# A graph-message kernel on one core: a third of the node normalization goes to GpSimd, and its source gathers get another gate

## The chip, the core and the metric

The kernel runs on one core of a Trainium2 chip. The metric is device time in microseconds, the median of several executions. Engines: TensorE (PE), VectorE (DVE), ScalarE (ACT), GpSimd (POOL), and SyncE (SP), which here only issues DMAs.

## What is computed

25,000 edges send messages between 100,000 nodes of 128 features, all float32. `dst` is sorted.

```python
src, tgt = (x[row], x[col])
msg_input = jnp.concatenate([src, tgt, edge_attr], axis=-1)
h = jax.nn.relu(msg_input @ W1 + b1)
msg = h @ W2 + b2
attn_weight = jax.nn.sigmoid(jnp.concatenate([msg, conf], axis=-1) @ Wa + ba)
out = jax.ops.segment_sum(msg * attn_weight, col, num_segments=x.shape[0])
x = _layernorm(x + out, axis=-1)   # over the 128 features, eps 1e-5
```

Every node is normalized, the many without a message too.

## The kernel before, in words

**Edges.** 49 steps (`STEPS`, index k) of 512 edges (four groups of 128) each. 16 are *near* steps, for edges with low target numbers: their target rows come by plain DMA and a one-hot matmul ("pick"), and their sums go into a block `near` in SBUF ("place"). 33 are *list* steps: GpSimd gathers source rows (L658) and target rows (L669) by indirect DMAs, four of each in a step; sums run along each partition and land in `stash`, from where GpSimd scatters finished rows to `out` (L679, four DMAs for a list step, from step 15 on; the last eleven list steps' scatters come behind step 48's gather). `RING` = 4 buffers hold the gathered rows.

In step k TensorE turns (transposes) source rows, target rows and edge attributes into PSUM (L878, L883 or L892, L897); each of the three raises `turned_ps_ready` by one. ScalarE copies them to SBUF (L758), TensorE does the hidden layer (L904), ScalarE relu (L763), TensorE the messages (L914). VectorE adds biases (L1383, L1386), ScalarE does the sigmoid and gates (L767, L773), and VectorE (list) or TensorE and VectorE (near) sum. TensorE's order is written out: hidden(k), sums of k-1, turn(k+1), messages(k). ScalarE's: relu(k), turn(k+1), norms, gates(k), norms.

**Nodes.** All nodes beyond the near block pass through SBUF in 63 chunks of 128 partitions x 11 rows, three chunks to a batch b, one batch in two steps, 21 batches. Six slots (`SLOTS`) hold them, so a batch reuses the slots of the one two back. SP loads a chunk (L485), VectorE takes statistics (L1187), `batch_scales(b)` on VectorE works out two scalars a row in step 2b (L1168 to L1179; `sc` has two halves, used in turn), and the rows are normalized in place. `ACT_ROWS = (7, 7, 8)` says how many of each chunk's 11 rows ScalarE does (L777, `norm_chunk`); VectorE does the rest (L1229, `norm_rows`). `normed` counts 2 for a chunk when both are done. SP then stores it (L543) and, once that has landed, reloads the slot.

**SP** goes through one list in order. In iteration k, once turn(k) has ended: attributes of k+4, near loads for k+3 and k+2; in an even k reloads of chunks 0 and 1 of batch k/2+1, near blocks, then the store of chunk 2 of batch k/2-1; in an odd k the reload of chunk 2 of batch (k+1)/2, then the stores of chunks 0 and 1 of batch (k-1)/2.

**GpSimd** also has one list: 115 groups of four indirect DMAs: gathers of steps 0 and 1, then for each k from 2 the source gather, the target gather if k is a list step, and the scatters that `SCATTERS` puts there. `gather_src(k)` waits until the first part of turn k-4 is done (the buffer is free). In every second group, ahead of its third DMA (its second in a group behind a scatter), `pause` waits until the group before has landed.

Of the kernel before, what the change touches and what calls it, by code (L numbers as in the profile page):

```python
# [15 lines left out]
RING = 4  # L16
SLOTS = 6
# [53 lines left out]
HEAD_STEP = {l: STEP_OF[(S_, LG * (l + 1) - 1)] + 1 for l in range(LISTS)}  # L71
TAIL_STEP = {l: STEP_OF[(S_, LG * l)] + 1 for l in range(1, LISTS)}
V_STEP = 7
ACT_ROWS = (7, 7, 8)
NEAR_ACT = 6
BESIDE = 8
SSTEPS = 9
# [12 lines left out]
def is_list(k):  # L90
    return 0 <= k < K and STEPS[k][0] == S_
# [35 lines left out]
EXTRAS = [u for u in USES if u[0] != D_]  # L127


def list_groups_of(b):  # L130

    return [STEPS[k - 1][1] for k in (2 * b - 1, 2 * b) if is_list(k - 1)]
# [16 lines left out]
def columns(b):  # L149

    at, n = {}, 0
    if 3 * b < 63:
        at["nodes"] = n
        n += even(ROWS) + (2 * ROWS if crosses(b) else 2 * even(ROWS))
    for i in list_groups_of(b):
        at[i] = n
        n += G
    if b in NEAR_OUT:
        at["near"] = n
        n += even(NEAR_OUT[b][1] - NEAR_OUT[b][0])  # L160
    return at, n


COLS = [columns(b)[0] for b in range(BATCHES)]
WIDTH = [columns(b)[1] for b in range(BATCHES)]
WIDEST = max(WIDTH)
# [15 lines left out]
def build(nc, x, src, dstw, attr, conf, W1, b1, W2, b2, Wa, ba, out):  # L182
# [9 lines left out]
    with ExitStack() as ctx:  # L192
# [234 lines left out]
        def wait(eng, semaphore, value):  # L427
            if value > 0:
                eng.wait_ge(semaphore, value)
# [188 lines left out]
        def _(pool):  # L618
# [21 lines left out]

            def pause(j):
                landed, value, behind = latest
                if j == behind and groups[0] % PAUSE == PAUSE - 1:
                    pool.wait_ge(landed, value)

            def group_begun(landed, value, behind):
                groups[0] += 1
                latest[:] = landed, value, behind

            def gather_src(k):  # L650
                kind, i = STEPS[k]
                if k >= RING:

                    pool.wait_ge(turned_ps_ready, 3 * (k - RING) + 1)
                idx = table(src_list, i) if kind == S_ else src_near[:, i * G:(i + 1) * G]
                for j in range(G):
                    pause(j)
                    pool.indirect_dma_start(  # L658
                        out=rows_src[:, k % RING, j, :], out_offset=None, in_=x[:, :],
                        in_offset=bass.IndirectOffsetOnAxis(ap=idx[:, j:j + 1], axis=0),  # L660
                    ).then_inc(src_got[k % RING], 16)
                group_begun(src_got[k % RING], 16 * G * (k // RING + 1), 2)
# [89 lines left out]
        @block.scalar  # L752
        def _(act):
            def turn(k):
                for c in range(3):

                    act.wait_ge(turned_ps_ready, 3 * k + c + 1)
                    act.activation(turned[:, k % 2, c], turn_ps[:, c], ACT.Copy).then_inc(turned_ready, 1)  # L758

            def relu(k):  # L760

                act.wait_ge(hid_ps_ready, k + 1)
                act.activation(hid[:, k % 2], hid_ps[:], ACT.Relu, bias=b1_col[:, 0:1]).then_inc(hid_ready, 1)  # L763

            def gates(k):
                act.wait_ge(logit_ready, k + 1)
                act.activation(weight[:, k % 2], logit[:, k % 2], ACT.Sigmoid).then_inc(weight_ready, 1)  # L767
                act.wait_ge(raw_ready, k + 1)


                act.wait_ge(weight_ready, k + 1)
                for j in range(G):
                    act.activation(gated[:, k % 2, j, :], raw[:, k % 2, j, :], ACT.Copy,  # L773
                                   scale=weight[:, k % 2, j:j + 1]).then_inc(gated_ready, 1)

            def norm(row, b, col, parts=P):
                return act.activation(row, row, ACT.Identity, scale=sc[0:parts, b % 2, 0, col:col + 1],  # L777
                                      bias=sc[0:parts, b % 2, 1, col:col + 1])

            def norm_chunk(b, i):  # L780
                c = chunk_of_batch(b, i)
                if c is None:
                    return
                act.wait_ge(scale_ready, 2 * (b + 1))
                n = chunk_parts(c)
                for r in range(ACT_ROWS[i]):
                    last = norm(nodes[0:n, c % SLOTS, r, :], b, node_column(b, i, r), n)
                last.then_inc(normed[c % SLOTS], 1)

            def norm_list(b, i):  # L790
                act.wait_ge(scale_ready, 2 * (b + 1))
                for j in range(G):
                    row = stash[:, list_slot(i) + j, :]
                    last = norm(row, b, COLS[b][i] + j)
                last.then_inc(out_ready, 1)

            def norm_near(b):
                act.wait_ge(scale_ready, 2 * (b + 1))
                low, high = NEAR_OUT[b]
                for r in range(min(NEAR_ACT, high - low)):  # L800
                    last = norm(near[:, low + r, :], b, COLS[b]["near"] + r)
                last.then_inc(near_normed, 1)

            act.wait_ge(consts_in, 16 * 8)
            turn(0)
            for k in range(K + 3):
                if k < K:
                    relu(k)
                if k + 1 < K:
                    turn(k + 1)  # L810
                b = (k - 1) // 2
                if k % 2:
                    norm_chunk(b, 0)
                elif k:
                    norm_chunk(b, 2)
                if k < K:
                    gates(k)
                if k == 0 or b >= BATCHES:
                    continue
                if k % 2:  # L820
                    norm_chunk(b, 1)
                    for i in list_groups_of(b)[:1]:
                        norm_list(b, i)
                    if b in NEAR_OUT:
                        norm_near(b)
                else:
                    for i in list_groups_of(b)[1:]:
                        norm_list(b, i)
                    act.sem_inc(scale_free, 1)

            def general():
                with act.Fori(1, T + 1) as nth:
                    act.wait_ge(any_turn_ps, nth)
                    for c in range(3):
                        last = act.activation(turned[:, 0, c, 0:P], turn_ps[:, c, 0:P], ACT.Copy)
                    last.then_inc(any_turned, 1)
                    act.wait_ge(any_hid_ps, nth)
                    act.activation(hid[:, 0, 0:P], hid_ps[:, 0:P], ACT.Relu, bias=b1_col[:, 0:1]).then_inc(any_hid, 1)
                    act.wait_ge(any_raw, nth)
                    act.activation(any_weight[:], g_raw[:, F:F + 1], ACT.Sigmoid, bias=any_lin[:, 0:1]  # L840
                                   ).then_inc(any_weighed, 1)
                    act.wait_ge(any_weighed, nth)
                    act.activation(g_gated, g_raw[:, 0:F], ACT.Copy, scale=any_weight[:, 0:1]).then_inc(any_gated, 1)

            act.wait_ge(flag_ready, 1)
            with act.If(act.value_load(unsorted[0:1, 0:1], min_val=0, max_val=1) > 0):
                general()
            act.nop()
# [161 lines left out]
        def _(dve):  # L1010
# [188 lines left out]
            def norm_rows(b, some):  # L1199
                return [(norm_row, b, i, r) for i in some if chunk_of_batch(b, i) is not None  # L1200
                        for r in range(ACT_ROWS[i], ROWS)]

# [47 lines left out]
            def near_norm_rows(b):  # L1250
                if b not in NEAR_OUT:
                    return []
                low_, high_ = NEAR_OUT[b]
                return [(near_norm_row, b, high_, r) for r in range(low_ + NEAR_ACT, high_)]
# [17 lines left out]
            def batch_scales(b, beside):  # L1272
                n = STATS_BEFORE[b + 1]
                dve.wait_ge(stat_ready, n)
                wait(dve, scale_free, b - 1)
                if not WIDTH[b]:
                    do(beside)
                    dve.sem_inc(scale_step, SSTEPS)
                    dve.sem_inc(scale_ready, 2)
                    return  # L1280
                scales(stats[:, b % 2, 0:WIDTH[b], :], sc_calc[:, :, 0:WIDTH[b]], sc[:, b % 2, :, 0:WIDTH[b]], scale_step, SSTEPS * b,
                       scale_ready, beside)
# [120 lines left out]
            for k in range(K + 3):  # L1403
# [25 lines left out]
                    add_v()  # L1429
                if is_near(k):  # L1430
                    make_place(k)
                under = norm_rows(b - 1, (2,)) + near_norm_rows(b - 1) if k % 2 == 0 else []
                if b - 1 == BATCHES - 1:
                    near_norms(b - 1)
                if (k % 2 == 0 or k == K) and b < BATCHES and k <= K:
# [101 lines left out]
```

## Time and profile before

| | us |
|---|---|
| median of 3 runs | 699.24 |
| lowest and highest | 695.41, 699.42 |
| the profiled execution | 698.01 |
| its span | 696.3 |
| busy: GpSimd, VectorE, ScalarE, TensorE | 460.0, 460.3, 426.6, 400.3 |

The span is the time from the first to the last instruction of the profiled execution. Busy times don't count waits, register and semaphore instructions, or the issue of DMAs by SP. The issue of an indirect DMA by GpSimd counts as busy.

### The profile page before, as it was taken

The page shows a single profiled execution, that of the slowest core. Times are in us where ns is not written, and L with a number is a line of the kernel's source. Part 1 is how long each engine was busy: PE and PEld are TensorE (multiplying, and loading weights), DVE is VectorE, ACT ScalarE, POOL GpSimd, SP SyncE. Part 2 cuts the span into 40 slices and gives each one's busy share as a digit, 9 for nine tenths or more (in the row PEclk, how much of TensorE's full clock was granted, in tenths as well). Part 3 has the DMA queues.
Part 4 walks back from the last instruction along what each step waited for, and adds up shares of the span by engine and source line. Part 5 has one row for each costly group of instructions (what it writes and reads, how often), then busy time and mean ns, then how long its engine had stood idle before and what let it go on. Part 6 is the DMA issues. An engine that isn't in the chain of part 4 may idle for free. (4 is left out here: it accounts for less than half of the span.)

```text
span 696.3 us, 7976 instructions
## 1 busy us (share of the span) xinstructions
PE 400.3 (57%) x1902; PEld 286.0 (41%) x1902; DVE 460.3 (66%) x1555; ACT 426.6 (61%) x1089; POOL 460.0 (66%) x473
## 2 busy tenths in 40 slices
PE   1776884656738547384472967194744647498200
PEld 0454653434526336263351645062523535376100
DVE  4877886996694848678386779668575764555300
ACT  0354997699667937495373968586773769455200
POOL 7666665665667666675664766666756777677772
PEclk9998997787787959697696889697885977789555
DMA  6979788999885957768677679878485755731310
GB/s 159 366 225 330 250 308 286 331 297 334 291 288 153 316 181 264 261 193 289 192 243 261 217 251 302 284 251 297 154 304 179 243 179 166 200 94 47 102 48 18
DMA packets 79874, 159.30 MB, mean 229 GB/s; under 512 B 13970, under 2 KB 48086, under 8 KB 79826
## 3 DMA queue, kind: packets, MB, share of 16 engines
q1 hardware_dynamic: 65106, 129.47, 54.9%
q0 software_dynamic: 14720, 29.32, 14.7%
q8 instruction: 15, 0.25, 0.2%
q14 instruction: 33, 0.27, 0.1%
HBM read 99.75 MB, written 59.95 MB: 229 GB/s over the span
## 5 line engine op out<-in xcount | busy, mean ns | idle before, releaser
L777 ACT ACTIVATE nodes<-nodes,sc 128x128 f32<-128x128 f32 (+1 forms) x462 | 184.0, 485 | 0.0
L758 ACT ACTIVATE turned<-turn_ps 128x512 f32<-128x512 f32 x147 | 81.1, 591 | 167.8 <-PE turn_ps L878 92.9
L669 POOL DMA_INDIRECT rows_dst<-x,dst_list x132 | 129.5, 981 | 74.1 <-DMA rows_src<-x,src_list 35.7
L679 POOL DMA_INDIRECT out<-stash,row_idx x132 | 136.1, 1031 | 63.6 <-issue 35.6
L658 POOL DMA_INDIRECT rows_src<-x,src_list x132 | 129.1, 978 | 64.3 <-issue 36.4
L904 PE MATMUL hid_ps<-turned,w 128*128 128x512 f32 x294 | 158.5, 681 | 2.7 <-ACT turned L758 2.6
L1187 DVE BATCH_NORM_STATS2 stats<-nodes 128x6 f32<-128x256 f32 (+1 forms) x358 | 133.5, 418 | 17.0 <-DMA nodes<-x 17.0
L878 PE MATMUL turn_ps<-ident,rows_src 128*128 128x128 f32 x196 | 36.5, 317 | 109.3 <-DMA rows_src<-x,src_list 102.6
L914 PE MATMUL msg_ps<-w2x,hid 128*128 128x129 f32 x392 | 71.5, 341 | 36.6 <-ACT hid L763 36.6
L904 PEld LDWEIGHTS hid_ps<-turned,w 128*128 128x128 f32 x294 | 62.2, 228 | 65.0 <-issue 59.2
L914 PEld LDWEIGHTS msg_ps<-w2x,hid 128*128 128x128 f32 x392 | 65.0, 250 | 40.3 <-ACT hid L763 40.3
L1383 DVE TENSOR_TENSOR logit<-msg_ps,lin 128x4 f32<-128x4 f32 x49 | 7.7, 157 | 110.1 <-PE msg_ps L914 110.0
L878 PEld LDWEIGHTS turn_ps<-ident,rows_src 128*128 128x128 f32 x196 | 26.3, 161 | 129.7 <-DMA rows_src<-x,src_list 112.4
L658 POOL DMA_INDIRECT rows_src<-x,src_near x64 | 63.3, 989 | 21.8 <-issue 18.9
L1229 DVE TENSOR_SCALAR nodes<-nodes,sc 128x128 f32<-128x128 f32 (+1 forms) x231 | 69.6, 357 | 0.0
L773 ACT ACTIVATE gated<-raw,weight 128x128 f32<-128x128 f32 x196 | 62.6, 390 | 9.9 <-DVE raw L1386 7.2
L883 PE MATMUL turn_ps<-ident,rows_dst 128*128 128x128 f32 x132 | 28.5, 354 | 67.5 <-DMA rows_dst<-x,dst_list 67.5
L938 PE MATMUL sum_ps<-gated,place 128*128 128x128 f32 x384 | 56.6, 294 | 12.5 <-ACT gated L773 6.0
L938 PEld LDWEIGHTS sum_ps<-gated,place 128*128 128x128 f32 x384 | 49.5, 199 | 27.2 <-issue 15.5
L1347 DVE TENSOR_TENSOR near<-near,sum_ps 128x512 f32 (+3 forms) x64 | 34.9, 546 | 36.9 <-PE sum_ps L938 27.9
L777 ACT ACTIVATE stash<-stash,sc 128x128 f32<-128x128 f32 x132 | 53.9, 479 | 0.0
L1304 DVE SCALAR_TENSOR_TENSOR acc<-acc,keep,gated 128x128 f32<-128x128 f32 x129 | 43.7, 339 | 10.6 <-ACT gated L773 9.6
(139 smaller groups left out, 477.2 us busy)
## 6 DMA issues: line engine op xcount, KB each, us to landing
nodes<-x SPq DMA_DIRECT2D x62, 704.0 KB, 6.8
out<-nodes SPq DMA_DIRECT2D x62, 704.0 KB, 4.3
attr_in<-edge_attr SPq DMA_DIRECT2D x49, 256.0 KB, 5.4
near_dst<-line SPq DMA_DIRECT2D x16, 256.0 KB, 6.3
near_x<-x SPq DMA_DIRECT2D x20, 192.0 KB, 4.4
near_x<-x SPq DMA_DIRECT2D x24, 128.0 KB, 4.5
out<-near SPq DMA_DIRECT2D x4, 704.0 KB, 6.6
rows_src<-x,src_list POOLq DMA_INDIRECT x132, 4.3
```

The lines of the kernel that those rows point to most:

```text
L658: pool.indirect_dma_start(out=rows_src[:, k % RING, j, :], out_offset=None, in_=x[:, :], in_offset=bass.IndirectOffsetOnAxis(ap=idx[:, j:j ...
L669: pool.indirect_dma_start(out=rows_dst[:, i % RING, j, :], out_offset=None, in_=x[:, :], in_offset=bass.IndirectOffsetOnAxis(ap=column(dst ...
L679: pool.indirect_dma_start(out=out[:, :], out_offset=bass.IndirectOffsetOnAxis(ap=column(row_idx, i, j), axis=0), in_=stash[:, list_slot(i) ...
L758: act.activation(turned[:, k % 2, c], turn_ps[:, c], ACT.Copy).then_inc(turned_ready, 1)
L773: act.activation(gated[:, k % 2, j, :], raw[:, k % 2, j, :], ACT.Copy, scale=weight[:, k % 2, j:j + 1]).then_inc(gated_ready, 1)
L777: return act.activation(row, row, ACT.Identity, scale=sc[0:parts, b % 2, 0, col:col + 1], bias=sc[0:parts, b % 2, 1, col:col + 1])
L878: last = pe.transpose(turn_ps[:, 0, j * P:(j + 1) * P], rows_src[:, s, j, :], ident[:])
L904: last = pe.matmul(hid_ps[:], w1[:, c, :], turned[:, k % 2, c, :], start=(c == 0), stop=(c == 2))
L914: last = pe.matmul(msg(j), hid[:, k % 2, j * P:(j + 1) * P], w2x[:], start=True, stop=True)
L938: last = pe.matmul(sum_ps[:, use % 2, w * P:(w + 1) * P], place[:, b * P:(b + 1) * P], gated[:, k % 2, j, :], start=True, stop=True)
L1187: return dve.bn_stats(st.rearrange("p w k -> p (w k)"), pair)
L1229: ins = dve.tensor_scalar(nodes[0:n, u, r, :], nodes[0:n, u, r, :], sc[0:n, b % 2, 0, col:col + 1], sc[0:n, b % 2, 1, col:col + 1], ALU.mu ...
```

## The change

1. `ACT_ROWS` becomes `(7, 7)`: neither ScalarE nor VectorE normalizes a batch's third chunk. GpSimd does its 11 rows with `tensor_scalar`. They are spread over the places behind each odd group of GpSimd's list that belongs to step 2b+3 or 2b+4 (2 or 3 places a batch, 3 to 6 rows each). The first row in a place waits for the batch's scales; the last row of the chunk raises `normed` by 2.
2. A group whose predecessor in the list had rows put in front of it doesn't pause.
3. `gather_src(k)` waits, from k = 2 on, for all three parts of turn k-2.
4. Before VectorE writes the scales of batch b it waits until GpSimd has finished the third chunk of batch b-2.

```diff
-ACT_ROWS = (7, 7, 8)
+ACT_ROWS = (7, 7)
...
+def group_steps():
+    at = [0, 1, 0, 1]
+    for k in range(2, K):
+        at += [k] * (1 + is_list(k) + len(SCATTERS.get(k, ())))
+    return at
+
+def third_rows_places():
+    at, places = group_steps(), {}
+    for b in range(21):
+        behind = [n + 1 for n, k in enumerate(at) if n % 2 and k in (2 * b + 3, 2 * b + 4)]
+        for q, n in enumerate(behind):
+            places[n] = (b, ROWS * q // len(behind), ROWS * (q + 1) // len(behind))
+    return places
...
+THIRD_ROWS = third_rows_places()
...
             def pause(j):
                 landed, value, behind = latest
-                if j == behind and groups[0] % PAUSE == PAUSE - 1:
+                if j == behind and groups[0] % PAUSE == PAUSE - 1 and groups[0] - 1 not in THIRD_ROWS:
                     pool.wait_ge(landed, value)
 
             def group_begun(landed, value, behind):
                 groups[0] += 1
                 latest[:] = landed, value, behind
+                if groups[0] in THIRD_ROWS:
+                    third_rows(*THIRD_ROWS[groups[0]])
+
+            def third_rows(b, low, high):
+                c = chunk_of_batch(b, 2)
+                u, n = c % SLOTS, chunk_parts(c)
+                pool.wait_ge(scale_ready, 2 * (b + 1))
+                for r in range(low, high):
+                    col = node_column(b, 2, r)
+                    last = pool.tensor_scalar(nodes[0:n, u, r, :], nodes[0:n, u, r, :], sc[0:n, b % 2, 0, col:col + 1],
+                                              sc[0:n, b % 2, 1, col:col + 1], ALU.mult, ALU.add)
+                if high == ROWS:
+                    last.then_inc(normed[u], 2)
 
             def gather_src(k):
                 kind, i = STEPS[k]
-                if k >= RING:
-
-                    pool.wait_ge(turned_ps_ready, 3 * (k - RING) + 1)
+                if k >= 2:
+                    pool.wait_ge(turned_ps_ready, 3 * (k - 2) + 3)
...
                 if k % 2:
                     norm_chunk(b, 0)
-                elif k:
-                    norm_chunk(b, 2)
...
                 wait(dve, scale_free, b - 1)
+                if b > 1 and chunk_of_batch(b - 2, 2) is not None:
+                    c = chunk_of_batch(b - 2, 2)
+                    dve.wait_ge(normed[c % SLOTS], 2 * (c // SLOTS + 1))
...
-                under = norm_rows(b - 1, (2,)) + near_norm_rows(b - 1) if k % 2 == 0 else []
+                under = near_norm_rows(b - 1) if k % 2 == 0 else []
```

## Rows read from the trace of the kernel before

**Rows 1.** The page, part 1: busy us (share of the span) x instructions.

```profile
PE 400.3 (57%) x1902; PEld 286.0 (41%) x1902; DVE 460.3 (66%) x1555; ACT 426.6 (61%) x1089; POOL 460.0 (66%) x473
```

**Rows 2.** The page, part 5: busy us, mean ns of one, idle before, its releaser.

```profile
L777 ACT ACTIVATE nodes<-nodes,sc 128x128 f32<-128x128 f32 (+1 forms) x462 | 184.0, 485 | 0.0
...
L669 POOL DMA_INDIRECT rows_dst<-x,dst_list x132 | 129.5, 981 | 74.1 <-DMA rows_src<-x,src_list 35.7
L679 POOL DMA_INDIRECT out<-stash,row_idx x132 | 136.1, 1031 | 63.6 <-issue 35.6
L658 POOL DMA_INDIRECT rows_src<-x,src_list x132 | 129.1, 978 | 64.3 <-issue 36.4
...
L658 POOL DMA_INDIRECT rows_src<-x,src_near x64 | 63.3, 989 | 21.8 <-issue 18.9
L1229 DVE TENSOR_SCALAR nodes<-nodes,sc 128x128 f32<-128x128 f32 (+1 forms) x231 | 69.6, 357 | 0.0
```

**Rows 3.** The chain that ended last, in order of time: start us, us, what.

```profile
678.22 0.30 issue
...
683.63 0.97 POOL out L679
```

**Rows 4.** Waits of GpSimd from 45 to 610 us: total us, times, longest.

```profile
POOL rows_dst L669 <- DMA rows_src<-x,src_list: 35.7, 14, 4.2
...
POOL rows_src L658 <- DMA out<-stash,row_idx: 19.6, 6, 6.5
POOL out L679 <- DMA out<-stash,row_idx: 16.9, 5, 4.8
POOL out L679 <- DMA rows_src<-x,src_near: 8.9, 5, 2.4
POOL rows_src L658 <- DMA rows_dst<-x,dst_list: 6.3, 3, 3.1
```

**Rows 5.** Timeline of GpSimd, 0 to 4 us: start us, us, instruction, idle before.

```profile
1.25 0.20 POOL L622 MEMSET upper<- 128x128 f32 x1
1.39 0.19 POOL L623 MEMSET ones_all<- 128x128 f32 x1
...
2.32 0.28 POOL L630 TENSOR_SCALAR_AFFINE_SELECT shift<-shift 128x128 f32<-128x128 f32 x1
2.56 0.28 POOL L632 TENSOR_SCALAR_AFFINE_SELECT corner<-corner 128x128 f32<-128x128 f32 x1
3.03 1.12 POOL L658 DMA_INDIRECT rows_src<-x,src_list  x1 [0.18 <-issue]
```

**Rows 6.** Timeline of VectorE and of GpSimd, 228 to 231 us.

```profile
228.38 1.75 DVE L1361 TENSOR_TENSOR pick<-near_dst,node_of 128x1536 f32<-128x1536 int32 x1
...
229.00 1.98 POOL L679 DMA_INDIRECT out<-stash,row_idx  x1 [0.30 <-issue]
```

**Rows 7.** Timeline of GpSimd at step 6's gather, and of TensorE at turn 4.

```profile
64.38 0.94 POOL L658 DMA_INDIRECT rows_src<-x,src_list  x1 [0.30 <-issue]
...
66.50 3.41 PE L938 MATMUL sum_ps<-gated,place 128*128 128x128 f32 x16 [4.01 <-DVE near L1347]
69.70 0.93 PE L878 MATMUL turn_ps<-ident,rows_src 128*128 128x128 f32 x4
...
70.90 0.60 PE L897 MATMUL turn_ps<-ident,attr_in 128*128 128x128 f32 x4
```

**Rows 8.** Timeline: last target gather and turn of step 16, gather of step 18.

```profile
208.88 0.94 POOL L669 DMA_INDIRECT rows_dst<-x,dst_list  x1 [0.30 <-issue]
...
212.36 1.06 PE L897 MATMUL turn_ps<-ident,attr_in 128*128 128x128 f32 x4
...
220.11 0.95 POOL L658 DMA_INDIRECT rows_src<-x,src_near  x1 [0.30 <-issue]
```

**Rows 9.** Timeline of SP: batch 7's third store; of VectorE: batch 9's scales.

```profile
228.15 0.34 SPq L543 DMA_DIRECT2D out<-nodes  x1
...
249.60 0.20 DVE L1179 SCALAR_TENSOR_TENSOR sc<-stats,sc_calc 128x42 f32<-128x42 f32 x1
```

## The prediction

> **What bounds the kernel now.** I read the page first. GpSimd and VectorE are busy for the same 460 us of a span of 696.3 us, so shares alone don't say which one decides [rows 1]. The second look is at GpSimd's groups: nearly all of its time is 460 indirect DMAs of 0.94 to 0.98 us each, and they begin at once and end at the end: the chain that ended last is nothing but the last scatters, each 0.97 us behind a gap of 0.30 us, up to 684.6 us [rows 2, 3]. The third look is at what GpSimd waits for. Only two kinds of gap are there: 0.30 us of "issue" before nearly every DMA, and waits of up to 6.5 us for a DMA of its own [rows 4]. It never waits for TensorE or VectorE by more than the usual gap. So GpSimd's own stream is the bound: 460 x (0.95 + 0.30) = 575 us, about 22 us by which some DMAs are stretched, and the waits. TensorE waits for its gathers, and what TensorE, ScalarE and VectorE save or lose in busy time is off the path as long as they keep up.
>
> The waits for its own DMAs are the pauses: before one DMA of every second group of four, GpSimd waits until the group before has landed. From 45 to 610 us they are 35.7 + 19.6 + 16.9 + 8.9 + 6.3 = 87.4 us in 14 + 6 + 5 + 5 + 3 = 33 places, of which 33 x 0.30 = 9.9 us is the gap that stays: 77.5 us [rows 4].
>
> **The change, part by part.**
>
> *Pauses gone.* A pause is skipped if rows were put in front of the group before it. Rows go behind every odd group of steps 3 to 44: 47 places. The pauses skipped are those from the group issued at 46.6 us to the one that ends at 607.1 us, which is the stretch just summed: -77.5 us. The three ahead of it stay, and so do those among the last scatters, which cost nearly nothing.
>
> *Rows added on GpSimd.* 21 batches x 11 rows = 231 tensor_scalar instructions of 128 x 128, 3 to 6 in a place, with two scalars per partition. The trace has none. Nearest is GpSimd's affine select of the same shape, one read and one write of SBUF: 0.282 us each, but started every 0.24 to 0.25 us, and start to start is what a stream pays [rows 5]. A memset, which only writes, starts every 0.145 us. So a read costs about 0.10 us more. Below: the row costs what the select costs, 0.245 us. Above: two scalars are two more reads that overlap nothing, 0.445 us. I take half of one more read, 0.295 us, since it is nearest to the select and small reads may overlap.
>
> To that comes VectorE. A scatter that GpSimd began at 229.00 us, under VectorE's pick (two operands in SBUF), took 1.98 us where a scatter takes 0.97, and ended 0.85 us behind the pick [rows 3, 6]. Over all DMAs the groups sum to 136.1 + 129.5 + 129.1 + 63.3 = 458.0 us, while 328 x 0.94 + 132 x 0.97 = 436.4: 21.6 us of stretch, 0.047 us each [rows 2]. I charge a row the same, with 0 as the lower end. So 0.342 us a row, 231 x 0.342 = +79.0 us. The step from a DMA to a row and back I set to nothing: last select to first DMA was a gap of 0.19 us against 0.30 between DMAs [rows 5], and a row ahead of a DMA may add or save 0.3 us in each place, 14 us either way at the most.
>
> [...]
>
> *Rows removed elsewhere.* ScalarE loses 8 x 21 = 168 rows at 485 ns (81 us), VectorE 3 x 21 = 63 at 357 ns (22 us) [rows 2]. Both wait for TensorE, which waits for gathers, so this is worth nothing on the path; the cover is GpSimd's stream itself.
>
> *The gate of the source gathers.* Before, step k's gather waited for the first third of turn k-4; now for all three of turn k-2. Behind it on GpSimd's queue are everything else of the step, its target gathers, rows and scatters. Where it binds is the start. Step 6's gather was issued at 64.38 us, but turn 4 ran only at 69.70 to 71.5 us, as it stood in TensorE's queue behind a sum that waited for VectorE's near block (whose load was late) [rows 7]. The new stream would arrive at 64.4 - 2.3 (one pause gone) + 16 x 0.342 (rows so far) = 67.6 us and wait until 71.5: +3.9 us, and it never gets that back, since it is the bound. Later it doesn't bind: at step 18, turn 16 ended with the attribute part 212.36 + 1.06 = 213.4 us, 3.6 us behind the end of its last target gather (208.88 + 0.94), and the gather of step 18 was issued at 220.11 [rows 8]. Between a step's last target gather and the gate lie eight DMAs of the step between and 5 or 6 rows, 10 + 2 = 12 us to cover landing and turning; step 16 needed under 4 us of them.
>
> *Rows wait for the scales; stores wait for the rows.* The scales of batch 9 were ready at 249.8 us [rows 9], and GpSimd reaches the place of its first rows some 25 us later, two steps on: nothing. The store of the third chunk now waits for GpSimd. SP issues in order, so its next attribute load, near load and reload stand behind. Batch 7's store went out at 228.15 us and its slot was reloaded for batch 9 [rows 9]. GpSimd has its last rows of batch 7 in front of step 19's gather, at about 240 us, so the store comes some 13 us later and the reload some 10. The stats of batch 9 were due for scales that were ready at 249.8 us, and become some 9 us late, but the next thing that VectorE has to do there (the bias of step 18) only comes after TensorE's turn 19, at 257 us. Most batches are shifted by under 8 us. I take 0; up to 3 us in each of the five batches whose last rows lie behind a near step's scatters, 15 us, is the upper end.
>
> **Sum.** -77.5 + 79.0 + 3.9 = +5.4 us on the profiled execution (698.01 us, of which 696.3 is span): 703.4. The median shown is 1.2 us above that execution, so I forecast 704 us for the median, against 699.24. About 1% (7 us) is what a measurement can tell here, so this is "no change" leaning to slower. With 0.292 a row (select plus block) it is 67.5 + 4.7 - 77.5 = -5; with 0.392 (a full extra read) 90.6 + 3.1 - 77.5 = +16: own range 693 to 716 us.
>
> **Rivals.**
>
> 1. *Rows are as cheap as the select.* For: the same shape and traffic, pitch 0.245 us, and no block in the four of them. Against: they ran in the first 3 us, beside almost nothing on VectorE, and took no scalar per partition. 231 x 0.245 = 56.6, gate then 71.5 - (62.1 + 3.9) = 5.5: -15.4 us, 684 us. With rows that also fill part of the 0.30 us gap, down to 676.
>
> 2. *Scalars are full reads (the other side).* Place: every row on GpSimd. Price 0.445 + 0.047 = 0.492 us, 113.7 us; gate 1.5; +37.7 us, 737 us. It decides from (77.5 - 4) / 231 = 0.318 us a row on: above that the rows cost more than the pauses. For: the 0.10 us step between memset and select. Against: the scalars are one element per partition and could be asked for with the row itself. [...]
>
> 3. *The gate or SP's queue takes the pauses' place.* Late stores make reloads late, VectorE's stats wait, turns are late, and GpSimd stands at the gate. It decides once turn k-2 ends more than 12 us behind step k-2's last gather. 15 us over the forecast: 719 us. For: SP works through one queue in order, and the stores stand in it. Against: the 3.6 us at step 16, and that messages of a step come behind the next turn anyway.
>
> 4. *Pauses come back as stretch*: without them the DMAs in flight slow each other. Then the change gives nothing back and +79 us remain. Against: unpaused groups of up to 12 DMAs in a row ran at 0.30 us gaps. I give it under 1 in 50 and count it with rival 2.
>
> **How the numbers follow.** Forecast 0.35, cheap rows 0.32, full reads 0.21, gate or SP 0.12. The forecast's range splits into 0.02 faster by over 1%, 0.20 within, 0.13 slower; cheap rows are faster; full reads slower; rival 3 is 0.04 within, 0.08 slower. That gives 0.34 faster, 0.24 same, 0.42 slower. The range that holds 8 in 10 takes in both ends of the row's cost: 679 to 736 us.
>
> **What would show it.** GpSimd's new group at about 0.30 us start to start between blocks, 231 of them, 60 to 110 us busy; no waits of GpSimd on its own DMAs between 45 and 600 us; one wait of some 4 us on TensorE before step 6's gather; ScalarE down by 81 us and VectorE by 22; the stores of the third chunks issued later. Wrong if waits on TensorE of several us recur, if the scales show up as a releaser of GpSimd, if the pitch is outside 0.24 to 0.50 us, or if the DMAs themselves grow beyond 1.0 us.

## The result, and the profile after

The kernel after takes 733.1 us (median of 4 runs, 731.3 to 734.92) against 698.1 us (median of 4, 695.41 to 699.42) for the kernel before in the same comparison: ratio 1.0506, 95% interval 1.0461 to 1.0552. It is slower by 5%. Medians here and below are over all executions of a kernel, ratios and intervals only over those that weren't in a slower state, so a ratio can differ a little from that of the two medians. The range that was to hold 8 in 10 (679 to 736) holds the time. The forecast of 704 and its own range (693 to 716) miss it; rival 2, at 737, was the nearest.

| profiled execution | before | after |
|---|---|---|
| span, us | 696.3 | 730.5 |
| GpSimd busy | 460.0 | 574.1 |
| ScalarE busy | 426.6 | 366.1 |
| VectorE busy | 460.3 | 458.8 |

The page of the kernel after, part 1 (busy us, share of the span, instructions), answers to [rows 1]:

```profile
PE 400.4 (55%) x1902; PEld 291.2 (40%) x1902; DVE 458.8 (63%) x1492; ACT 366.1 (50%) x921; POOL 574.1 (79%) x704
```

GpSimd has 231 instructions more and 114 us more of work. Its groups, from the list of groups on GpSimd with shapes kept apart (answers to [rows 2]):

```profile
L711 POOL DMA_INDIRECT out<-stash,row_idx x132 | 134.8, 1021 | 39.4 <-issue 37.2 <-DMA out<-stash,row_idx 2.2
L690 POOL DMA_INDIRECT rows_src<-x,src_list x132 | 129.4, 980 | 43.4 <-issue 36.1 <-PE turn_ps L927 3.9 <-DMA rows_src<-x,src_near 1.9
L701 POOL DMA_INDIRECT rows_dst<-x,dst_list x132 | 127.6, 967 | 40.4 <-issue 38.1 <-DMA rows_dst<-x,dst_list 2.4
L678 POOL TENSOR_SCALAR nodes<-nodes,sc 128x128 f32<-128x128 f32 x220 | 109.4, 507 | 1.7
L690 POOL DMA_INDIRECT rows_src<-x,src_near x64 | 65.3, 1021 | 18.8 <-issue 18.5 <-PE turn_ps L927 0.3
L678 POOL TENSOR_SCALAR nodes<-nodes,sc 96x128 f32<-96x128 f32 x11 | 5.5, 530 | 0.1
```

The DMAs cost what they cost before (457.1 us in all, 458.0 before). What is new is the L678 group: 115.0 us on the page for 231 rows, 0.498 us each, where the sum had 0.342. How such a block looks in the timeline of GpSimd (start us, us, instruction, idle before):

```profile
93.23 0.94 POOL L701 DMA_INDIRECT rows_dst<-x,dst_list  x1 [0.31 <-issue]
94.22 2.17 POOL L678 TENSOR_SCALAR nodes<-nodes,sc 128x128 f32<-128x128 f32 x5
96.55 0.98 POOL L690 DMA_INDIRECT rows_src<-x,src_list  x1 [0.16 <-issue]
...
106.69 3.07 POOL L678 TENSOR_SCALAR nodes<-nodes,sc 128x128 f32<-128x128 f32 x6
109.92 0.98 POOL L690 DMA_INDIRECT rows_src<-x,src_list  x1 [0.16 <-issue]
```

The shortest blocks of five take 2.17 us again and again, of three 1.31, of four 1.74: a start every 0.43 us. I read these as undisturbed. Other blocks of five take up to 2.93. A row block and the DMA behind it are 0.16 us apart and the block follows its DMA after about 0.04: 0.20 us where two DMAs are 0.30 apart.

All waits of GpSimd that are more than the usual gap, of the kernel after (total us, times, longest), answer to [rows 4]:

```profile
POOL rows_src L690 <- PE turn_ps L927: 4.2, 3, 2.4
POOL rows_dst L701 <- DMA rows_dst<-x,dst_list: 2.4, 1, 2.4
POOL out L711 <- DMA out<-stash,row_idx: 2.2, 5, 0.7
POOL rows_src L690 <- DMA rows_src<-x,src_near: 1.9, 1, 1.9
POOL rows_src L690 <- DMA rows_src<-x,src_list: 1.1, 1, 1.1
```

The 77.5 us of pauses are gone. The gate held GpSimd for 2.40 us before step 6 (at 70.64 us). It also shows 1.46 us before step 3, but that gather starts almost where it did before (33.55 us, 33.38 before), so it cost next to nothing; behind step 6 it never holds GpSimd beyond a usual gap. So the span adds up: +115.0 (rows), -4.7 (47 x 0.10 of shorter gaps), -77.5 (pauses), +2.2 at step 6 (2.40 less the 0.16 that is usual behind a row block), -0.9 (DMAs) = +34.1 us; the spans differ by 34.2.

Off this path much has moved. SP's longest waits and VectorE's, of the kernel after:

```profile
SPq L562 <- POOL nodes L678: 203.0, 21, 17.9
SPq L562 <- ACT nodes L809: 148.6, 31, 11.4
...
DVE stats L1217 <- DMA nodes<-x: 61.3, 14, 8.4
```

SP now stands 203 us at the stores of the third chunks and 148.6 at the others; before, it stood 301.6 us at the stores, released by ScalarE's rows. So the stores wait some 50 us more than before, not 203, and VectorE waits 61.3 us for nodes (17.0 before). That is the queue effect of rival 3, and it is real, but GpSimd never waited for it: no scale is among its releasers, and the one turn that held it (step 6) was late in the kernel before too [rows 7].

### The profile page after: what moved, and what is told of

It reads as the page before. It is cut to its first block and busy times, and to the rows that moved or that the text cites. A ratio compares the mean times of both kernels' runs of the same rounds, so it can differ in the third digit from the quotient of the medians.

```text
span 730.5 us, 7977 instructions
## 1 busy us (share of the span) xinstructions
PE 400.4 (55%) x1902; PEld 291.2 (40%) x1902; DVE 458.8 (63%) x1492; ACT 366.1 (50%) x921; POOL 574.1 (79%) x704
## 5 line engine op out<-in xcount | busy, mean ns | idle before, releaser
L1217 DVE BATCH_NORM_STATS2 stats<-nodes 128x6 f32<-128x256 f32 (+1 forms) x358 | 133.4, 417 | 61.3 <-DMA nodes<-x 61.3
L701 POOL DMA_INDIRECT rows_dst<-x,dst_list x132 | 127.6, 967 | 40.4 <-issue 38.1
L934 PE MATMUL hid_ps<-turned,w 128*128 128x512 f32 x294 | 153.4, 662 | 2.5 <-ACT turned L790 2.5
L809 ACT ACTIVATE nodes<-nodes,sc 128x128 f32<-128x128 f32 x294 | 117.2, 482 | 0.0
L678 POOL TENSOR_SCALAR nodes<-nodes,sc 128x128 f32<-128x128 f32 (+1 forms) x231 | 115.0, 509 | 1.8
L908 PE MATMUL turn_ps<-ident,rows_src 128*128 128x128 f32 x196 | 39.6, 338 | 139.2 <-DMA rows_src<-x,src_list 111.9
L908 PEld LDWEIGHTS turn_ps<-ident,rows_src 128*128 128x128 f32 x196 | 28.2, 172 | 160.3 <-DMA rows_src<-x,src_list 124.6
L934 PEld LDWEIGHTS hid_ps<-turned,w 128*128 128x128 f32 x294 | 60.1, 220 | 61.4 <-issue 56.0
L690 POOL DMA_INDIRECT rows_src<-x,src_near x64 | 65.3, 1021 | 18.8 <-issue 18.5
L944 PE MATMUL msg_ps<-w2x,hid 128*128 128x129 f32 x392 | 69.3, 335 | 14.3 <-ACT hid L795 14.3
L913 PEld LDWEIGHTS turn_ps<-ident,rows_dst 128*128 128x128 f32 x132 | 19.8, 182 | 97.5 <-DMA rows_dst<-x,dst_list 97.4
```

Of the source, the lines that this page charges most:

```text
L678: last = pool.tensor_scalar(nodes[0:n, u, r, :], nodes[0:n, u, r, :], sc[0:n, b % 2, 0, col:col + 1], sc[0:n, b % 2, 1, col:col + 1], ALU. ...
L690: pool.indirect_dma_start(out=rows_src[:, k % RING, j, :], out_offset=None, in_=x[:, :], in_offset=bass.IndirectOffsetOnAxis(ap=idx[:, j:j ...
L701: pool.indirect_dma_start(out=rows_dst[:, i % RING, j, :], out_offset=None, in_=x[:, :], in_offset=bass.IndirectOffsetOnAxis(ap=column(dst ...
L908: last = pe.transpose(turn_ps[:, 0, j * P:(j + 1) * P], rows_src[:, s, j, :], ident[:])
L934: last = pe.matmul(hid_ps[:], w1[:, c, :], turned[:, k % 2, c, :], start=(c == 0), stop=(c == 2))
L944: last = pe.matmul(msg(j), hid[:, k % 2, j * P:(j + 1) * P], w2x[:], start=True, stop=True)
```

## The experiments

Each ratio is to the kernel before on the same chip in the same comparison. The first four runs below ran together.

**The pauses alone.** The kernel before, without the same 47 pauses and with the new gate; ScalarE and VectorE still normalize all three chunks.

```diff
-                if j == behind and groups[0] % PAUSE == PAUSE - 1:
+                if j == behind and groups[0] % PAUSE == PAUSE - 1 and groups[0] - 1 not in THIRD_ROWS:
...
-                if k >= RING:
-                    pool.wait_ge(turned_ps_ready, 3 * (k - RING) + 1)
+                if k >= 2:
+                    pool.wait_ge(turned_ps_ready, 3 * (k - 2) + 3)
```

> Kernel before with two parts of the change only: the same 47 pauses gone and the gate on turn k-2. ScalarE and VectorE still normalize all three chunks. Theory (GpSimd's stream is the bound, the pauses are pure cost): 698 - 77.5 + about 6 for the gate = 627 us, GpSimd idle only in gaps of 0.30 us. Rival (the pauses' time is needed by somebody else, so it comes back as waits at the gate or as late turns): 650 us or more, with GpSimd waiting for TensorE at many steps.

Measured: 633.1 us against 702.1, ratio 0.9045 (0.8998 to 0.9091). From the page of this run and its waits on GpSimd:

```profile
PE 395.2 (63%) x1902; PEld 280.9 (45%) x1902; DVE 460.8 (73%) x1555; ACT 425.8 (68%) x1089; POOL 458.1 (73%) x473
```

```profile
POOL rows_src L676 <- issue: 57.9, 190, 0.3
POOL rows_dst L687 <- issue: 39.0, 128, 0.3
POOL out L697 <- issue: 38.1, 125, 0.3
POOL rows_src L676 <- PE turn_ps L915: 10.7, 3, 9.5
```

The busy time of every engine is that of before within 2%; only the waiting is gone. GpSimd waits at the gate (9.5 us the longest time, before step 6) and at the first pauses, which were kept, and otherwise stands in its 0.30 us gaps. Nobody needed the pauses' time here: TensorE, ScalarE and VectorE keep up with the full stream. So the change has two parts with opposite signs: about -69 us for pauses with the gate, about +100 us for the rows (733.1 against 633.1, from two comparisons). The rows' own time is 115.0 us; they get back 4.7 in shorter gaps, and about 7 because GpSimd reaches step 6 later and waits 2.4 us at the gate in place of 9.5. That leaves 103, the difference of the two profiled spans (730.5 and 627.0).

**The same with the old gate.**

```diff
-                if k >= 2:
-                    pool.wait_ge(turned_ps_ready, 3 * (k - 2) + 3)
+                if k >= RING:
+                    pool.wait_ge(turned_ps_ready, 3 * (k - RING) + 1)
```

> As the run above, but with the old gate (first part of turn k-4). Theory: the gate costs only at the start, so 4 to 8 us less than the run above. Rival (without pauses the gate is what paces GpSimd): 20 us or more apart, or slower than with the gate because DMAs in flight slow each other (GpSimd's DMAs above 1.0 us, landing above 6 us).

Measured: 631.3 us, ratio 0.8982 (0.8942 to 0.9021). The two intervals overlap: what the gate costs here isn't told apart from nothing, and a cost of 20 us is excluded. The waits of GpSimd show where the 9.5 us went:

```profile
POOL rows_dst L688 <- DVE stash L1342: 9.2, 4, 3.1
```

Without the gate GpSimd runs ahead until all four buffers of target rows are full, and then waits for VectorE's sums to free one, at four places between 108 and 158 us. So in this trace the gate moved a wait and added hardly any. The DMAs are slower by 2%: the mean gather is 1.00 us (0.98 before), the mean scatter 1.05 (1.03), far from what the rival needs.

**The kernel after with the old gate** (the same edit in the kernel after).

> Kernel after, only its gate set back to the first part of turn k-4. Theory: the gate costs 2.4 + about 1.5 us at the start of the stream and nothing later: 729 us against 733. Rival (the gate costs along the whole way): under 720 us.

Measured: 730.7 us, ratio 1.0406 (1.0376 to 1.0435), against 1.0506 (1.0461 to 1.0552) for the kernel after in its own comparison. By the two intervals the gate is worth 2 to 12 us, and the two comparisons were separate. The traces put it at the lower end: step 6's gather starts at 68.21 us here and at 70.64 in the kernel after, 2.4 us. The rival, under 720 us, is out. The rows take 112.6 us in this trace.

**Constants in place of the scalars.** GpSimd's rows multiply by 1.5 and add 0.25; this leaves out the layer norm of the third chunks.

```diff
-                    last = pool.tensor_scalar(nodes[0:n, u, r, :], nodes[0:n, u, r, :], sc[0:n, b % 2, 0, col:col + 1],
-                                              sc[0:n, b % 2, 1, col:col + 1], ALU.mult, ALU.add)
+                    last = pool.tensor_scalar(nodes[0:n, u, r, :], nodes[0:n, u, r, :], 1.5,
+                                              0.25, ALU.mult, ALU.add)
```

> Kernel after, but GpSimd's 231 rows multiply and add two constants in place of each row's two scalars (so the third chunks come out with other values). Theory (the two scalars are what lifts a row from 0.24 to 0.43 us): rows start every 0.25 us, 231 x 0.18 = 42 us less, about 691 us. Rival (GpSimd's two-operation arithmetic itself is that slow): pitch 0.40 or more and 728 us or more.

Measured, in a single execution: 687.0 us, against 702.1 for the kernel before. The group on the page and two blocks in the timeline of GpSimd:

```profile
L678 POOL TENSOR_SCALAR nodes<-nodes 128x128 f32<-128x128 f32 (+1 forms) x231 | 64.5, 314 | 0.9
```

```profile
92.88 1.35 POOL L678 TENSOR_SCALAR nodes<-nodes 128x128 f32<-128x128 f32 x5
94.39 0.98 POOL L690 DMA_INDIRECT rows_src<-x,src_list  x1 [0.16 <-issue]
...
104.15 1.66 POOL L678 TENSOR_SCALAR nodes<-nodes 128x128 f32<-128x128 f32 x6
```

The rows fall from 115.0 to 64.5 us, 0.279 us each. So the multiplication and addition on 128 columns are not what makes a row slow; the two scalars per partition are. With rows this cheap the change comes out as rival 1 had it, 15 us under the kernel before, as far as a single execution can tell. The rival of this run (slow arithmetic, 728 us or more) falls.

**Forms of a row, alone and beside VectorE.** The kernel before, with blocks of GpSimd instructions behind its last DMA; some of them while VectorE runs a series of its own.

```diff
+            bench(8, lambda t: pool.tensor_scalar(w[:, t, :], w[:, t, :], s0, s1, ALU.mult, ALU.add))
+            bench(8, lambda t: pool.tensor_scalar(w[:, t, :], w[:, t, :], s0, 0.25, ALU.mult, ALU.add))
+            bench(8, lambda t: pool.tensor_scalar(w[:, t, :], w[:, t, :], s0, None, ALU.mult))
+            bench(8, lambda t: pool.tensor_scalar(w[:, t, :], w[:, t, :], 1.5, 0.25, ALU.mult, ALU.add))
+            bench(8, lambda t: pool.tensor_copy(w[:, t, :], w[:, t, :]))
...
+            both(1)
+            both(2)
+            both(3)
```

> Kernel before, with blocks of GpSimd instructions of 128x128 added behind its last DMA, when nothing else runs: 8 rows each with two scalars per partition, one scalar and a constant, one scalar alone, two constants, a copy, two scalars on 64 columns, two scalars on 256 columns, and an addition of two tensors. Then three blocks of 16 two-scalar rows while VectorE runs 24 scalar_tensor_tensor (two SBUF inputs), 24 tensor_scalar, 16 batch-norm statistics. Theory (each scalar is a read of its own of about 0.09 us; two-input instructions of VectorE block the rest): starts every 0.43, 0.34, 0.34, 0.25, 0.25 us; 64 columns about 0.38, 256 columns about 0.54; beside scalar_tensor_tensor 0.50 us or more, beside statistics 0.43. Rival (the second scalar is free, or the pitch follows the two operations): 0.43 for one scalar too, or 0.34 for two constants with two operations against 0.25 for the copy.

Measured, from the timeline of GpSimd; the last three are the blocks beside VectorE's scalar_tensor_tensor, tensor_scalar and statistics:

```profile
743.92 3.45 POOL L731 TENSOR_SCALAR nodes<-nodes,sc 128x128 f32<-128x128 f32 x8 [11.31 <-DMA out<-near]
747.47 2.79 POOL L732 TENSOR_SCALAR nodes<-nodes,sc 128x128 f32<-128x128 f32 x8
750.36 4.67 POOL L733 TENSOR_SCALAR nodes<-nodes,sc 128x128 f32<-128x128 f32 x8
755.12 2.13 POOL L734 TENSOR_SCALAR nodes<-nodes 128x128 f32<-128x128 f32 x8
757.32 1.94 POOL L735 COPY nodes<-nodes 128x128 f32<-128x128 f32 x8
759.36 2.98 POOL L736 TENSOR_SCALAR nodes<-nodes,sc 128x64 f32<-128x64 f32 x8
762.44 2.16 POOL L737 TENSOR_SCALAR nodes<-nodes,sc 128x256 f32<-128x256 f32 x4
...
766.58 8.55 POOL L744 TENSOR_SCALAR nodes<-nodes,sc 128x128 f32<-128x128 f32 x16 [0.21 <-POOL nodes L738]
775.36 7.87 POOL L744 TENSOR_SCALAR nodes<-nodes,sc 128x128 f32<-128x128 f32 x16 [0.23 <-POOL nodes L744]
783.46 6.88 POOL L744 TENSOR_SCALAR nodes<-nodes,sc 128x128 f32<-128x128 f32 x16 [0.23 <-POOL nodes L744]
```

Block time over count: two scalars 3.45 / 8 = 0.43 us, one scalar and a constant 0.35, two constants 0.27, copy 0.24. So with two operations each scalar in place of a constant costs 0.08 us more. Twice the columns add 0.11 (0.54), half of them save 0.06 (0.37): by these slopes about three quarters of a row's 0.43 us don't depend on its length, an estimate. VectorE's first two series beside GpSimd's blocks:

```profile
766.45 6.81 DVE L1490 SCALAR_TENSOR_TENSOR turned<-hid,sc 128x128 f32<-128x128 f32 x24 [27.05 <-POOLq L741]
775.32 6.30 DVE L1496 TENSOR_SCALAR turned<-hid,sc 128x128 f32<-128x128 f32 x24 [2.06 <-POOLq L741]
```

Beside VectorE's scalar_tensor_tensor, with two SBUF inputs, the row takes 8.55 / 16 = 0.53 us; beside VectorE's tensor_scalar 0.49; beside its statistics 0.43, as alone. The first two are means with an undisturbed tail, as VectorE ended 1.9 and 1.6 us before GpSimd's block. With the tail taken off at 0.43 us a row, it is about 0.57 and 0.51 us while both ran, an estimate. All that was expected but two things: one scalar without a second operation took 0.58, not 0.34, and tensor_scalar on VectorE slows the rows too.

**Every pause gone, and the gate alone**, first time.

```diff
-                if j == behind and groups[0] % PAUSE == PAUSE - 1:
+                if False:
```

> Kernel before with the new gate and every pause gone, the first three and those among the last scatters too. Theory (pauses are only cost): 3 to 9 us less than the run with 47 pauses gone, about 626 us. Rival (the last scatters, 44 DMAs in a row, need the pauses, or the queue of DMAs in flight slows them): no gain, or DMAs of GpSimd above 1.1 us among the last scatters.

> Kernel before with the new gate alone, pauses and norms as they were. Theory (the gate binds at steps 6 and 7 only): +6 us, about 1.01 of before. Rival (the gate is in the way of the pauses' slack too): +15 us or more.

These two ran, with the forms above, on a chip where the kernel before took 765.2 us (13 runs, 753 to 773). No pauses at all came to 766.2 (ratio 1.0068, 0.9987 to 1.015), the gate alone to 746.2 (0.9714, 0.9642 to 0.9786). The second is outside what either theory gave, and the first shows nothing of the gain. The waits of the run without pauses are not this kernel's usual ones:

```profile
ACT turned L757 <- remote: 115.1, 29, 28.8
PEld hid_ps L903 <- issue: 102.4, 206, 6.6
PEld sum_ps L937 <- issue: 98.8, 35, 19.9
...
POOL rows_src L657 <- PE turn_ps L896: 86.1, 14, 12.0
```

TensorE stood up to 19.9 us at a time with nothing recorded to wait for, ScalarE up to 28.8 behind something outside the records, and GpSimd waited 86.1 us for TensorE at the gate (16.3 us in the same kernel on the chip of the runs below). Here GpSimd's stream isn't the bound; the standing of the other engines is, as far as these waits tell. What makes that chip stand still stays open, and so does why the gate alone gained 3% there. The kernel before has no trace from that chip, and no run there had the pauses gone with the old gate, so how much of the lost gain is the gate's is open too. A row with two scalars takes 0.43 us there as in the kernel after, so I keep the table of forms and repeated the rest.

**The same again, elsewhere.**

> The run with the 47 pauses gone, once more, beside the next two: 0.90 of before. If it is near 1 here, its gain hangs on the chip and not on the kernel.

> Every pause gone, new gate. Theory (pauses are only cost): 3 to 9 us less than with 47 pauses gone. Rival (the last scatters need their pauses, or DMAs in flight slow each other): no gain.

> New gate alone, pauses and norms as before. Theory (it binds at steps 6 and 7 only): 1.00 to 1.01 of before. Rival (it binds along the way): 1.02 or more.

Measured together, the kernel before at 699.0 us: 47 pauses gone 632.7 us, 0.9108 (0.9024 to 0.9192), so the first result repeats. Every pause gone 631.1 us, 0.9065 (0.898 to 0.9149): 1.6 us apart, not told apart from nothing, and the 3 us of the theory neither shown nor excluded by the times. The wait for the gate in its trace says why so little came of it:

```profile
POOL rows_src L657 <- PE turn_ps L896: 16.3, 2, 13.5
```

With 47 pauses gone it was 10.9 us: most of what the first three pauses had cost (2.6, 2.5 and 0.9 us) comes back at the gate, since turns 0 and 4 aren't ready earlier. The gate alone 700.5 us, 1.0072 (1.0022 to 1.0123): 2 to 9 us, as expected. The kernels without pauses beat both the kernel before and the kernel after, by about 68 and 100 us. The gain held on the two chips where 47 pauses were taken out; on the third only the version without any pause ran, and it gained nothing.

## Why the prediction was right or wrong

**The bound** was right. GpSimd's stream sets the time, before and after: 34.1 of the 34.2 us are found in its own work and waits, and taking out only its waits took 69 us off the kernel (627 expected, 633.1 measured). That holds for the chips of these runs; on the chip with 765.2 us it didn't.

**Pauses, -77.5 us**: right. The run with the pauses alone gives -69 us with the gate in it; in its trace the gate holds 10.7 us, where its expectation had about 6.

**The rows, +79.0 us**: this is the term that was mis-sized. They measured 115.0. The step that failed is "I take half of one more read, 0.295 us, since it is nearest to the select and small reads may overlap". The forms show no such saving: the first scalar added 0.08 us and the second another 0.08 (0.27, 0.35, 0.43 us). A row without VectorE's block is 0.43 us, against my upper end of 0.445, which was worked out from memset and select [rows 5]. That this end came so near is in part luck: its base was too low (0.245 for 0.27) and its read too dear (0.10 for 0.08). The trace had nearly the price of one read in it. I had the upper end worked out from it, and took a middle because nothing in the trace showed two scalars.

**The block by VectorE, 0.047 us a row**: right in kind, a little low. 115.0 - 231 x 0.43 = 15.7 us, 0.068 a row. Such rows were slower beside VectorE's scalar_tensor_tensor with two SBUF inputs at the end of the kernel (0.53 against 0.43). How much of the 15.7 us each kind of VectorE instruction causes wasn't separated. With constants in place of the scalars the rows in the same 47 places lost only 64.5 - 231 x 0.27 = 2 us. The stretched scatter of the prediction was no single case: in the kernel before seven DMAs of GpSimd take over 1.6 us, each began while a pick of VectorE ran, and each ended 0.80 to 0.87 us behind that pick.

**The step from a DMA to a row**, set to nothing: it saved 4.7 us, within the 14 either way.

**The gate, +3.9 us**: 2.2 at step 6 in the trace, since slower rows brought GpSimd there later, as the terms of rival 2 had it (1.5). Alone it measured +2 to +9 us. With the old gate and no pauses another wait stood in its place (9.2 us, for VectorE's sums), which the prediction didn't look for.

**Scales and stores, 0**: right on the path. VectorE's wait for nodes rose from 17.0 to 61.3 us, and it reached no wait of GpSimd.

**Rows removed elsewhere, 81 and 22 us**: off the path, as said, but too large. ScalarE's busy time fell by 60.5 us and VectorE's by 1.5. The 485 ns are the mean duration of one row, and neighbouring rows overlap: 462 of them make up 184.0 us of busy time, 0.40 us each [rows 2]. VectorE's group of rows fell by 20.3 us, from 69.6 to 49.3, but those rows had overlapped other work of VectorE (one from 247.07 us, 0.45 us long, with an instruction that began at 247.33), and other groups grew a little.

**Small things in the sum.** 698.01 + 5.4 + 1.2 is 704.6, where I wrote 704. Of the signs that I had named, the pitch came out at 0.498 us, just inside 0.24 to 0.50, and the rows' busy time at 115.0 us, outside 60 to 110.

**The rivals.** Rival 2 with 737 us came true to 4 us, with its own terms: 113.7 for the rows (115.0), 1.5 for the gate (2.2). Its row of 0.445 + 0.047 us was in truth 0.43 + 0.068, two errors that nearly cancel. It had 0.21 and should have had more. The turning point lies between the two rows measured: 0.498 us gave +5%, 0.279 gave 687 against 702. By the measured terms it is (77.5 + 4.7 + 0.9 - 2.2) / 231 = 0.35 us a row, an estimate, where the prediction had 0.318, since it left out the shorter gaps. Rival 3's queue effect exists and wasn't the bound. Rival 4 (without pauses DMAs slow each other) is out: with the 47 pauses gone the gathers' mean stayed at 0.98 us and the scatters' at 1.02 (1.03 before).

## What to carry to other kernels

When one engine's list is the bound, first take away what is waited for in it, alone, and only then think of filling the hole: here the hole was worth nearly 10% of the kernel's time and the filling cost about 14%. Work isn't free because an engine looks idle. In the run of forms most of a short GpSimd instruction's time didn't depend on its length (two scalars: 0.37, 0.43 and 0.54 us for 64, 128 and 256 columns), and two scalars per partition made a row of 0.27 us one of 0.43. Where two rows of a trace give the price of one read, multiply by the number of reads and don't split the difference: here that gave 0.445 us for the row of 0.43, and half of one read gave 0.295.

## What was not expected

- In the run of forms a GpSimd tensor_scalar with one scalar and no second operation started every 0.58 us, slower than with two scalars and two operations (0.43). With a second operation that takes a constant it was 0.35. Why stays open.
- Beside VectorE's tensor_scalar (128x128, float32, two scalars) GpSimd's rows took 0.49 us in place of 0.43 (about 0.51 while both ran, an estimate).
- On one of the chips the kernel before ran 9% longer than on the others. The trace of the version without pauses has standstills of TensorE up to 19.9 us there without a recorded reason, and the ranking of the versions that ran there changed.
